# Fixed regions per expert: routing a perceiver layer's rows inside the attention loop

## The reference, cut to what matters

```python
x = x + cross_attention(layernorm(x), ctx)       # 16 heads of 64, 257 keys, softmax
x = x + wkv_mix(layernorm(x))                    # time mixing over the 32 tokens
xf = layernorm(x).reshape(-1, 128)               # 4096 rows
logits = xf @ Wr.T + br                          # 8 experts
expert_idx = argmax(logits, axis=-1)
h = relu(einsum('td,efd->etf', xf, W1) + b1)     # 128 -> 512
y = einsum('etf,edf->etd', h, W2) + b2           # 512 -> 128
x = x + y[expert_idx, arange(4096)]
```

## Time and profile before

| | us |
|---|---|
| median of 3 runs (1008.99 to 1013.52) | 1011.18 |
| the profiled execution, its own time | 1011.71 |
| its span, first to last instruction | 1009.8 |
| around the span | 1.9 |

### The profile page before, as it was taken

How to read it: one execution, slowest core, us unless ns; L and a number is a source line. 1 busy time by engine, 2 the same in 40 slices (tenths; PEclk the granted TensorE clock), 3 DMA queues, 4 the chain that set the end, 5 groups by cost and what they waited for, 6 DMA issues and landing times.

```text
span 1009.8 us, 29818 instructions
## 1 busy us (share of the span) xinstructions
PE 865.2 (86%) x8554; PEld 719.2 (71%) x8554; DVE 833.3 (83%) x2343; ACT 684.9 (68%) x2029; POOL 781.2 (77%) x1237
## 2 busy tenths in 40 slices
PE   7989998999999999999999999999998371049995
PEld 6777787887878787878878787878776271036664
DVE  5799889999999999999999999999998657025653
ACT  3777777777778787777777787877775113037774
POOL 5788888898989898989889898989896503735564
PEclk9999999999999999999999999999999555559998
DMA  9111111111211111111111111111100930111110
GB/s 237 34 33 33 34 33 33 33 34 38 59 32 32 32 32 32 32 32 32 32 34 52 40 32 32 32 32 32 32 2 2 141 154 14 53 43 51 51 52 20
DMA packets 56835, 45.11 MB, mean 45 GB/s; under 512 B 8366, under 2 KB 54577, under 8 KB 56768
## 3 DMA queue, kind: packets, MB, share of 16 engines
q1 hardware_dynamic: 54464, 40.01, 16.1%
q0 software_dynamic: 2304, 4.25, 1.3%
HBM read 37.25 MB, written 7.52 MB: 44 GB/s over the span
## 4 chain that ended last, share of the span: by engine, by line
PE 54%; POOL 15%; DVE 14%; issue 11%; ACT 3%; DMA 1%; DVEq 0%; POOLq 0%; ACTq 0%; SPq 0%
PE bank L373 11%; PE bank L396 10%; PE bank L420 7%; PE bank L385 5%; PE bank L413 5%; POOL Pn L925 5%; PE bank L1372 3%; DVE nmax L783 3%; POOL sorted_rows L1235 3%; PE bank L1387 2%; DVE cs L839 2%; DVE ql L769 2%; PE bank L402 2%; DVE Tl L777 2%; POOL cT L916 1%
## 5 line engine op out<-in xcount | busy, mean ns | idle before, releaser
L925 POOL TENSOR_TENSOR Pn<-Pe,rsum 128x1028 f32<-128x1028 f32 x128 | 243.2, 1900 | 53.0 <-DVE rsum L798 52.4
L713 ACT ACTIVATE Pe<-bank,nmax 128x257 f32<-128x257 f32 x512 | 240.5, 474 | 38.8 <-DVE nmax L783 38.4
L783 DVE TENSOR_REDUCE nmax<-bank 128x1 f32<-128x257 f32 x512 | 200.8, 412 | 19.7 <-PE bank L373 19.5
L373 PE MATMUL bank<-cT,qh 96*128 96x257 f16 x1024 | 185.4, 275 | 29.9 <-ACT Pe L713 28.4
L702 ACT ACTIVATE Th<-bank 128x512 f16<-128x512 f32 x256 | 141.3, 595 | 48.5 <-PE bank L420 48.5
L777 DVE TENSOR_TENSOR Tl<-bank,Th 128x512 f16<-128x512 f32 x256 | 173.4, 678 | 0.5 <-ACT Th L702 0.4
L420 PE MATMUL bank<-identf,Pn 128*128 128x128 f32 x1024 | 148.9, 273 | 0.0
L373 PE MATMUL bank<-cT,ql 96*128 96x257 f16 x512 | 139.5, 272 | 0.0
L373 PEld LDWEIGHTS bank<-cT,qh 96*128 96x128 f16 x1024 | 90.2, 97 | 47.4 <-ACT Pe L713 19.0
L420 PEld LDWEIGHTS bank<-identf,Pn 128*128 128x128 f32 x1024 | 114.8, 141 | 6.1
L713 ACT ACTIVATION_READ_ACCUMULATOR Pe<-bank,nmax 128x1 f32 x512 | 102.9, 201 | 0.0
(11 more groups left out here) (213 smaller groups left out, 2454.0 us busy)
## 6 DMA issues: line engine op xcount, KB each, us to landing
rawT<-in_dram SPq DMA_DIRECT2D x32, 385.5 KB, 3.9
raw<-in_dram SPq DMA_DIRECT2D x32, 384.0 KB, 4.4
sorted_rows<-fill SPq DMA_DIRECT2D x1, 2620.0 KB, 21.2
xs<-sorted_rows SPq DMA_DIRECT2D x40, 65.5 KB, 1.8
R<-in_dram SPq DMA_DIRECT2D x4, 512.0 KB, 5.2
Z<-last_rows SPq DMA_DIRECT2D x128, 2.2 KB
w1r<-in_dram SPq DMA_DIRECT2D x4, 512.0 KB, 13.7
w2fr<-in_dram SPq DMA_DIRECT2D x4, 512.0 KB, 13.6
```

Of the source, the lines that this page charges most:

```text
L373: last = nc.tensor.matmul(bank[SB[t]][:, 0:M], w[:, par, b, t * P:(t + 1) * P], cT[:, s4, c, 0:M], start=(k == 0), stop=(k == 2))
L713: nc.scalar.activation(Pe[:, n_par(j + 1), t, :], bank[SB[t]][:, 0:M], ACT.Exp, bias=nmax[:, n_par(j + 1), t:t + 1], accum_out=sums[:, n_p ...
L783: nc.vector.tensor_reduce(nmax[:, n_par(j + 1), t:t + 1], bank[SB[t]][:, 0:M], AX.X, ALU.max, negate=True).then_inc(s_nmax, 1)
L925: nc.gpsimd.tensor_tensor(Pn[:, par, :, :], Pe[:, par, :, :], rsum[:, par, :].unsqueeze(2).broadcast_to([P, QT, M]), ALU.mult)\
```

## The change

- The sorted order is no longer compact. Expert e owns rows e x 4096 onward of `sorted_rows` (now 32,896 rows), so a row's place needs only the rank within its expert so far: `held` keeps the running counts.
- Third norm, logits, argmax, rank and the writes of a chunk stand in the loop, one iteration behind the chunk's mixing. ACT copies the transposed rows (`x3T`) at the end of j = 6; POOL makes the reciprocal deviation in j = -1 (seven small operations) and issues the two indirect DMAs of the chunk at the end of its j = 3 and 4; DVE has eleven small operations in j = 0, 1, 2, 3 and 6; PE has two transposes (j = 6), two logit matmuls (j = 0) and four rank matmuls (j = 2). The mixed rows go to `stage`, a single buffer of two groups, in place of R.
- The residual into `stage` (end of j = 5) waits until the writes of the chunk before have landed.
- `L12` moves from DVE to ACT, behind `act_mix` and `act_early`. DVE's residual L807 now waits for the L12 copy of its own step. `chi` moves from POOL to ACT, between `cT` and the third exponential.
- SP writes blank rows for each chunk within the loop (1.07 MB each, 16 times), and the small constants are loaded and built in the first iterations. Five iterations are unrolled in place of four.
- Behind the loop only the number of tiles per expert, each tile's first row (`base`) and the packed experts are computed; SP reads `base` from SBUF for each tile load.

```diff
+            if exists(n):                                   # act_step, behind act_mix, act_early
+                wait(nc.scalar, s_left, n + 1)
+                wait(nc.scalar, s_PV, n - 1)
+                nc.scalar.activation(L12[:, n_par(j), :], bankh[7][:, 0:P], ACT.Copy).then_inc(s_L12, 1)
+            act_route(it, j)
...
+                    act_chi(n + 4, (j + 4) % NC8, ((j + 4) // GB) % NP2, (j + 4) % GB)
...
-            if exists(n):                                   # dve_step
-                wait(nc.vector, s_left, n + 1)
-                wait(nc.vector, s_PV, n - 1)
-                nc.vector.tensor_copy(L12[:, n_par(j), :], bankh[7][:, 0:P]).then_inc(s_L12, 1)
             if exists(n - 5):
                 wait(nc.vector, s_y, n - 4)
+                wait(nc.vector, s_L12, n + 1 if n_static(n) is None else min(n + 1, B))
                 tile = X[:, bass.ds(g - (2 if jj == 0 else 1), 1), :].rearrange("p o c -> p (o c)")
                 nc.vector.tensor_tensor(tile, tile, bank[7][:, 512 - C:512], ALU.add).then_inc(s_res, 1)
...
                 wait(nc.vector, s_m["y"], c + 1)            # dve_mix_end, j == 5
-                xc = X[:, bass.ds(MG * c, MG), :]
-                nc.vector.tensor_tensor(xc, xc, bank[3][:, 0:MT].rearrange("p (t c) -> p t c", t=MG), ALU.add)\
+                wait(nc.vector, s_sorted, 16 * MG * c)
+                wait(nc.vector, s_m["x3t"], c)
+                nc.vector.tensor_tensor(stage[:, :, 0:C], X[:, bass.ds(MG * c, MG), :],
+                                        bank[3][:, 0:MT].rearrange("p (t c) -> p t c", t=MG), ALU.add)\
                     .then_inc(s_m["res"], 1)
...
+            if j == 0 and chunk(it, 4) is not None:         # dve_mix_end
+                c = it - 4
+                wait(nc.vector, s_m["rs3"], c + 1)
+                wait(nc.vector, s_m["lgm"], c + 1)
+                for t in range(MG):
+                    last = nc.vector.scalar_tensor_tensor(lg[:, t, :], bank[7][:, ROUTE + t * E:ROUTE + (t + 1) * E],
+                                                          stage[:, t, C + 2:C + 3], brb[:, :], ALU.mult, ALU.add)
...
+            if j == 3 and chunk(it, 4) is not None:         # pool_route, behind pool_mix
+                c = it - 4
+                wait(nc.gpsimd, s_sorted, 16 * MG * c)
+                wait(nc.gpsimd, s_m["pf"], c + 1)
+                nc.gpsimd.tensor_tensor(stage[:, :, C], stage[:, :, C], stride[:, :], ALU.add).then_inc(s_m["id"], 1)
+                nc.gpsimd.tensor_copy(pos[:, :], posf[:, :]).then_inc(s_m["pos"], 1)
...
+                nc.gpsimd.tensor_tensor(held[:, :, :], held[:, :, :], hot[:, :, :], ALU.add).then_inc(s_m["held"], 1)
+            if j in (3, 4) and chunk(it, 4) is not None:
+                t = j - 3
+                nc.gpsimd.indirect_dma_start(sorted_rows, bass.IndirectOffsetOnAxis(ap=pos[:, t:t + 1], axis=0),
+                                             stage[:, t, :], None, bounds_check=E * TOK - 1).then_inc(s_sorted, 16)
...
+                sp.wait_ge(s_fill, 16 * i)                  # SP, in its loop
+                sp.dma_start(region[bass.ds(i, 1), :, :, :].rearrange("o p e r -> (o p) e r"), blank).then_inc(s_fill, 16)
...
-            for g in range(G):                              # POOL, behind the loop
-                nc.gpsimd.indirect_dma_start(sorted_rows, bass.IndirectOffsetOnAxis(ap=pos[:, g:g + 1], axis=0),
-                                             R[:, g, :], None, bounds_check=NT * P - 1).then_inc(s_sorted, 16)
```

More of the change, by code:

```diff
@@ L676, in pe_mix @@
                 last.then_inc(s_m["y"], 1)
+            if j == 6 and chunk(it, 3) is not None:
+                c = it - 3
+                pe_mix_bank(it, j, n)
+                wait(nc.tensor, s_m["res"], c + 1)
+                for t in range(MG):
+                    last = nc.tensor.transpose(bank[3][:, t * P:(t + 1) * P], stage[:, t, 0:C], identf[:, :])
+                last.then_inc(s_m["x3t"], 1)
             if j == 1 and chunk(it, 2) is not None:
@@ L853, in dve_mix_a @@
         def dve_mix_a(it, j):
+            if j == 1 and chunk(it, 4) is not None:
+                c = it - 4
+                wait(nc.vector, s_m["lg"], c + 1)
+                nc.vector.tensor_reduce(mx[:, :], lg[:, :, :], AX.X, ALU.max).then_inc(s_m["mx"], 1)
+            if j == 2 and chunk(it, 4) is not None:
+                c = it - 4
+                wait(nc.vector, s_m["held"], c)
+                wait(nc.vector, s_m["mxw"], c + 1)
+                nc.vector.tensor_tensor(hot[:, :, :], wt[:, :, :], mxw[:, :].unsqueeze(2).broadcast_to([P, MG, E]),
+                                        ALU.is_equal).then_inc(s_m["hot"], 1)
+            if j == 3 and chunk(it, 4) is not None:
+                c = it - 4
+                wait(nc.vector, s_m["pos"], c)
+                wait(nc.vector, s_m["slot"], c + 1)
+                nc.vector.tensor_reduce(posf[:, :], slot[:, :, :], AX.X, ALU.add).then_inc(s_m["pf"], 1)
             if j in (3, 4) and chunk(it, 2) is not None:
@@ L881, in dve_mix_c @@
         def dve_mix_c(it, j):
+            if j == 6 and chunk(it, 3) is not None:
+                for t in range(MG):
+                    last = nc.vector.bn_aggr(stage[:, t, C + 1:C + 3], stats3[:, t, :])
+                last.then_inc(s_m["ag"], 1)
+            if j == 1 and chunk(it, 4) is not None:
+                c = it - 4
+                if n_static(it) == 4:
+                    wait(nc.vector, s_ftab, 10)
+                wait(nc.vector, s_m["eq"], c + 1)
+                nc.vector.tensor_tensor(wt[:, :, :], eq[:, :, :], desc[:, :].unsqueeze(1).broadcast_to([P, MG, E]),
+                                        ALU.mult).then_inc(s_m["wt"], 1)
             if j == 0 and chunk(it, 3) is not None:
@@ L1037, in drain_mix @@
                 step(LIT + 2, j)
+            for j in range(-1, 5):
+                step(LIT + 3, j)
         def time(a):
@@ L1267, in _ @@
                 act_cT(b, b, 0, b)
+            act.wait_ge(s_ctx[0], 16)
+            for b in range(GB - 1):
+                act_chi(b, b, 0, b)
             for c in range(GB):
@@ L1271, in _ @@
             drain_mix(act_step)
-            act_std()
-            for i in range(CH):
-                act.wait_ge(s_f["xT"], i + 1)
-                wait(act, s_f["rt"], i - 1)
-                nc.scalar.activation(x3T[:, i % 2, :], bank[4 * (i % 2)][:, :], ACT.Copy).then_inc(s_f["xc"], 1)
             for k in range(2 * E):
```

397 lines of the change are left out of this document (218 added, 179 removed).

## The result

| | before | after |
|---|---|---|
| median, us | 1011.46 (1008.99 to 1013.52, 4 runs) | 1023.27 (1022.12 to 1025.43, 4 runs) |
| after / before | | 1.0127, 95% interval 1.011 to 1.0144 |
| span of the profiled execution | 1009.8 | 1020.7 |

The two sides of the sum can be read off from three events: the last residual of the attention, the last mixing residual, the first expert matmul.

What follows compares the result with a forecast made beforehand. PE and DVE were taken to be at their limit in the attention loop. From 1011.7 us, -50 behind the loop and +65.6 in it gave 1027.3, or 1027 on the runs' scale; 8-in-10 range 986 to 1052.

Steps and rivals of the forecast that it cites:

- The two sides of the sum: Work behind the attention loop shrinks, -50 us; the loop's iterations and early steps get longer, +65.6 us.
- Main case: The forecast's own sum with no rival applying: 1027 us, range 1010 to 1044, chance 0.50.
- the ring: Waits closing through steps with act_mix: DVE's maximum, PE's fourth score part, ACT's mixing and L12 copies, DVE's residual L807.
- (a): Attention loop: ACT's L12 copy behind act_mix lengthens steps -1, 0, 1 and 3, +2.38 us an iteration, bounds 0 and 4.
- (b): Logit matmuls ahead of step 0's mixing matmul, plus small DVE logit operations: +0.67 us an iteration, bounds 0.3 and 2.
- (c): Residual at the end of step 5 waits for the previous chunk's second sorting write: +1.7 us an iteration, bounds 0 and 5.
- (d): POOL's lost and added loop work is level; SP's fills and loads cost nothing, up to 5 us if delaying a write.
- rival 2: Sorting writes land in time: no stall in (c), 5 us less in the drain, 1002 us; chance 0.13.
- Side one: Behind the attention loop: 61.7 us gained after the last mixing residual, 11.4 lost in the drain ahead; -50 us.
- Handoff absorbed: In the attention loop ACT's L12 copy is in time, so (a) costs nothing: 991 us, chance 0.17.
- Starved writes: Sorting writes wait for long DVE and POOL operations, 2.5 us per chunk, 14 times: +35, 1062 us; chance 0.15.

Runs made afterwards that it cites:

- after, both of these: Changed kernel with L12 copied on DVE again and sorting writes reading a buffer of their own that ACT fills: 965.08 us, ratio 0.9555.
- before, chi on ACT: Kernel before the change with only the chi copies moved from POOL to ACT: 1004.24 us, ratio 0.994.
- the write buffer: Changed kernel with ACT copying stage rows at the end of step 2 into a separate buffer that the sorting writes read: 1004.40 us, ratio 0.9939.

## Why the prediction held, step by step

- **Main case.** The handoff, routing on the ring and the write wait are all there, and the verdict has the sign and nearly the size. But both sides were off in ways that partly cancelled: the loop was 7.6 us cheaper than +65.6, the stretch behind it 3.4 us less of a gain than -50. Within an iteration (a) and (b) cost 0.29 and 0.57 more than forecast, (c) and (d) 0.7 and 0.3 less. That the iteration came out within 0.4 us of 51.1 is in part luck.
- **(a) Handoff**, forecast 2.38 an iteration and 36 in all: measured 2.7 and 40. Right, and the four steps named are the four that got longer. The same handoff cost 28 us in the kernel before, 34 in that kernel with chi on ACT, and 40 with the routing. In the kernel before it ended the scans' collision, which nobody had booked. In the kernel after it meets the routing of step 0 on the same ring: step 0 costs 0.92 there, 0.50 without the routing. `chi` was rightly left at nothing.
- **(b) Routing on the ring**, forecast 0.67 within 0.3 and 2: about 1.2, from "after, both of these" against "before, chi on ACT", and ACT's copies for the write buffer are in it. Steps 0 and 1 give 0.26 and 0.31, near the forecast. Step 6 gives 0.61 and was booked as cancelled, with 0.1 for PE's two transposes. It is those transposes. First "after, both of these", then "before, chi on ACT", at the end of step 6 (which began at 537.08 and 528.09):

```profile
540.81 0.60 PE L424 MATMUL bank<-identf,Pn 128*128 128x128 f32 x4
541.51 0.44 PE L759 MATMUL bank<-identf,stage 128*128 128x128 f32 x2
541.78 0.60 PE L424 MATMUL bank<-identf,Pn 128*128 128x128 f32 x4
542.35 0.39 PE L377 MATMUL bank<-cT,qh 96*128 96x257 f16 x2
```

```profile
531.82 1.04 PE L420 MATMUL bank<-identf,Pn 128*128 128x128 f32 x8
532.71 0.39 PE L373 MATMUL bank<-cT,qh 96*128 96x257 f16 x2
```

The scores that DVE's next maximum waits for begin 5.27 us into the step in place of 4.62. DVE's own new work there, the aggregation, moves it by 0.2 and is covered; the two statistics stood in that step before.
- **(c) Write wait**, forecast 1.7 an iteration: worth 1.0. The idle time in the rows is (22.8 - 4.32 - 5.06) / 10 = 1.34 us an iteration, inside the 1.1 to 1.6 that was worked out; what was added to it "with a small delay of POOL" had no row behind it, and a part of a stall is paid back when PE is the next to be late. Over the kernel rival 2 had 20 us for it in the loop and 5 in the drain. The write buffer gave 7.0 up to the last attention residual (9.9 with L12 on DVE) and 10.6 in the drain, so the sum was near and its parts were not.
- **(d) POOL level.** POOL's own balance was right: 310 us busy of 380 with iterations of 50.8, 335 with 46.4, make 41 us an iteration in both. What nobody had priced is what POOL does to DVE: taking `chi` off POOL, or shifting the phase of DVE against POOL, shortened the scans by 20 us over 380. Alone that was worth 6 us (the 1004.2 kernel). In the steps of the kernel after it stands in step 4, 5.08 in place of 6.38. The trace of before had it in view: four scans in 1.90 and four in 0.56 us within one step.
- **Iteration**: 46.40 - 0.32 (chi) + 1.24 + 1.00 + 2.67 = 50.99, against 50.78 measured and 51.1 forecast (the terms depend on their order: the write buffer is worth 0.79 with L12 on DVE, and with that the sum is 50.78). Over the kernel, by the starts of `den` (263.58 and, ten iterations on, 727.54 before; 273.52 and 780.34 after): up to iteration 5 +9.9 (forecast 13.4), eleven iterations of +4.28 (the mean of the first ten) and nearly that in the last, 47.0 together (52.3), and +1.0 at the end of the attention (0).
- **Side one.** Behind the last mixing residual 26.2 us, forecast 25.7; the 16 splits were 10.6 in place of 9.73. The drain grew by 14.6, forecast 11.4: between the last two residuals it is 12.25 against 6.83, +5.4 where 5.2 was said. What failed is in (d), which put SP's fills and loads at nothing, or up to 5 us if they delay a write, by the 12% of the loop's row. The weight loads run in the drain, where the DMA engines are busy 84% of the time from 843 to 853 us, and they delayed the writes by 4.1 us. With the loads later the drain is 36.52 us, 11.2 more than before, and near the 11.4.
- **Rivals.** Handoff absorbed: wrong, L911 is idle 85 us. Writes in time: wrong, 22.8 us. Starved writes: wrong, no write took POOL more than 1.25 us. The Trainium skill, "SBUF — State Buffer", section "SBUF: two separate sides", gives 3.1 us for such a DMA beside a VectorE copy. No run here has a write beside such a copy; beside DVE's scans and the other work of the loop the writes took 1.06 to 1.10 us of POOL, 0.98 with DVE idle.

## What to carry to other kernels

Before an operation is moved to an idle engine, look at what stands ahead of it in that engine's queue: a copy of 0.3 us behind an instruction that waits for PE cost 40 us, since DVE's next maxima hung on it. Where a transfer must land before a buffer is rewritten, copy the buffer on an engine with room rather than double the loop body. And where a short operation's mean duration is well above its best one in the same trace, look for a collision: a shift of phase may end it, and here that was worth 6 us.

## What the runs showed of the hardware

- A hardware loop whose body grew from one iteration to two lost 7 us at each of its four returns to the start, and 33 us in all, while its instructions were fetched again (queues q8 and q14: 77 packets in the kernel after, 180 with the doubled body).
- Four scans of 128 x 32 took 0.56 us with POOL idle, 1.90 beside three of its operations, and 0.56 beside a DMA issue on POOL, which took 1.10 in place of 0.98.
- The residual that waited for the sorting writes of chunk 12 came 6.6 us after the start of the last of them (845.52 to 852.10) beside eight loads of 512 KB, and 2.5 us after it (848.87 to 851.32) with the loads behind it.
- Two gains on the same collision did not add up: 1038.9 for L12, 1038.1 with chi as well.
